# Splitting the experts' up weights into two halves inside the decoder instead of inside the expert loop

## What is computed

```python
x = x + _L0_xattn_ref(_layernorm(x), ctx_1024, ...)   # decoder (self, then cross attention) and feed-forward
x = x + _L0_ffn_ref(_layernorm(x), gate_w, W1, W2, W3) # experts
x = x + _L1_xattn_ref(...)
x = x + _L1_ffn_ref(...)

def _L0_ffn_ref(x, gate_w, W1, W2, W3):
    ...
    h1 = jnp.einsum('td,ehd->teh', xf, W1)     # E, H, D = 8, 896, 256
    h3 = jnp.einsum('td,ehd->teh', xf, W3)
    mid = jax.nn.silu(h1) * h3
    out_all = jnp.einsum('teh,edh->ted', mid, W2)
    ...
```

## Time and profile before

| | us |
|---|---|
| median of 3 runs (1475.7, 1476.38, 1487.08) | 1476.38 |
| the profiled execution | 1489.41 |
| its span, first to last instruction | 1487.7 |

### The profile page before, as it was taken

One profiled execution on the slowest core, in us unless ns is written; L12 is line 12 of the kernel. 1 busy time (PEld: TensorE's weight loads), 2 busy tenths in 40 slices (PEclk: granted clock), 3 DMA queues, 4 the chain that ended last, 5 costly groups with the idle time before them and its releaser, 6 DMA issues. The chain is left out here.

```text
span 1487.7 us, 26152 instructions
## 1 busy us (share of the span) xinstructions
PE 1095.7 (74%) x9362; PEld 734.2 (49%) x9362; DVE 955.5 (64%) x2656; ACT 598.4 (40%) x1195; POOL 413.3 (28%) x579
## 2 busy tenths in 40 slices
PE   2687777777479920399999999940367785899998
PEld 1364444444268820277877777730234432455554
DVE  3646566777337640478888888845367762677776
ACT  1335555666455300366566566510045553000000
POOL 4235654333516637012112112146011100001000
PEclk9768889999889955699999999975579868899999
DMA  7323332422023332666666675326422212010000
GB/s 193 110 68 94 85 92 76 143 80 72 3 85 106 111 111 101 246 215 230 208 242 221 220 243 207 128 85 196 135 67 57 63 32 72 15 39 27 29 8 15
DMA packets 129701, 168.45 MB, mean 113 GB/s; under 512 B 13331, under 2 KB 106278, under 8 KB 126630
## 3 DMA queue, kind: packets, MB, share of 16 engines
q1 hardware_dynamic: 125990, 157.61, 32.6%
q0 software_dynamic: 3584, 9.18, 2.0%
HBM read 119.10 MB, written 47.45 MB: 112 GB/s over the span
## 5 line engine op out<-in xcount | busy, mean ns | idle before, releaser
L1802 PE MATMUL moe_ps_u<-moe_x_hl,moe_up_hl 128*128 128x256 f16 x1932 | 226.5, 276 | 39.9 <-DVE moe_up_hl L1878 31.6
L1802 PEld LDWEIGHTS moe_ps_u<-moe_x_hl,moe_up_hl 128*128 128x128 f16 x1932 | 184.5, 99 | 82.0 <-DVE moe_up_hl L1878 38.0
L2165 PE MATMUL mix_ps_e<-wr_hl,mix_u_hl 128*128 128x512 f16 x768 | 172.4, 380 | 0.0
L1928 POOL CAST moe_mid_hl<-moe_mid 128x256 f16<-128x256 f32 x161 | 68.7, 426 | 312.9 <-DVE moe_mid L1893 312.9
L1878 DVE SCALAR_TENSOR_TENSOR moe_up_hl<-moe_up_in,moe_up_hl 128x512 f16<-128x512 f32 x161 | 105.1, 686 | 54.6 <-ACT moe_up_hl L1851 54.6
L545 ACT ACTIVATE dec_probs<-dec_ps_t 128x768 f32<-128x768 f32 (+1 forms) x128 | 117.2, 916 | 51.5 <-PE dec_ps_t L447 51.1
L2277 DVE SCALAR_TENSOR_TENSOR mix_acc<-mix_ps_e,mix_shares,mix_acc 128x256 f32<-128x256 f32 x256 | 110.3, 477 | 39.3 <-PE mix_ps_e L2165 39.0
L1851 ACT ACTIVATE moe_up_hl<-moe_up_in 128x512 f16<-128x512 f32 x161 | 99.1, 619 | 62.3 <-DMA moe_up_in<-in_moe_w 62.3
L2165 PEld LDWEIGHTS mix_ps_e<-wr_hl,mix_u_hl 128*128 128x128 f16 x768 | 74.9, 98 | 83.3 <-issue 1.1
L1814 PE MATMUL moe_ps_y<-moe_down_hl,moe_mid_hl 128*128 128x256 f16 x966 | 109.0, 273 | 0.0
L1172 DVE TENSOR_REDUCE mem_neg_m<-mem_ps_s 128x2 f32<-128x512 f32 x128 | 82.2, 684 | 38.2 <-PE mem_ps_s L1024 37.5
(11 more groups left out here) (277 smaller groups left out, 1900.8 us busy)
## 6 DMA issues: line engine op xcount, KB each, us to landing
moe_up_in<-in_moe_w SPq DMA_DIRECT2D x23, 1792.0 KB, 7.4
moe_down_in<-in_moe_w SPq DMA_DIRECT2D x23, 896.0 KB, 4.6
dec_q_dram<-dec_q_hl SPq DMA_DIRECT2D x48, 128.0 KB, 2.0
dec_k_dram<-dec_k_hl SPq DMA_DIRECT2D x48, 128.0 KB, 2.0
dec_q_st<-dec_q_dram SPq DMA_DIRECT2D x64, 96.0 KB, 2.6
dec_k_st<-dec_k_dram SPq DMA_DIRECT2D x64, 96.0 KB, 2.6
xs<-zeros SPq DMA_DIRECT2D x8, 736.0 KB
moe_x_in<-xs SPq DMA_DIRECT2D x23, 256.0 KB, 4.3
```

Source lines behind the costliest of these rows:

```text
L1802: mm = nc.tensor.matmul(bank[:, m, :], up_hl[t.slot][:, w, m, dc, f * P:(f + 1) * P], x_hl[t.slot][:, x, dc, :], start=(dc == 0 and w == x ...
L1928: nc.gpsimd.tensor_copy(mid_hl[t.slot][:, HI, f, :], mid[:, f, :]).then_inc(mid_hi, 1)
L2165: mm = nc.tensor.matmul(ps_e[fill % RING][:, :, :], u_hl[t.slot][:, r, dc, k * P:(k + 1) * P], wr_hl[:, m, dc, 2 * q:2 * q + 2, :], start= ...
```

## The change

The up weights of all 8 experts are split once in the decoder, in 64 pieces of 128 x 448, two in each self step and six in each cross step, and stored as halves in a DRAM tensor `moe_hl`. For each piece SP loads it (`load_up`), ACT makes the high half (`up_high`, at the places HIGH_AT), DVE the low half (`up_low`, at LOW_AT), and SP stores both in the next step (`store_up`). In `experts` the split of the up weights is gone from ACT and DVE, `up_in` too; SP loads the halves from `moe_hl` straight into `up_hl`, once `go_up` of the tile that last used the slot is done (`u_filled`). Down weights are split per tile as before. In SP's step the load of the down weights now stands behind that of the up weights.

```diff
 def decoder(...):
+        UP_PIECES, SELF, CROSS = moe_up.shape[2] // PIECE, 2, 6
...
+        UPS, UP_RAWS, UP_SLOTS = ups_before[-1], 9, 8
+        HIGH_AT = {SELF: (2, 4), CROSS: (2, 3, 4, 5, 6, 7)}
+        LOW_AT = {SELF: (3, 5), CROSS: (3, 5, 5, 7, 7, 7)}
...
+                def load_up(n):
+                    if n >= UP_RAWS:
+                        sp.wait_ge(up_lo, n - UP_RAWS + 1)
+                    e, cols = up_at(n)
+                    sp.dma_start(up_raw[n % UP_RAWS][:, :], moe_up[e][:, cols]).then_inc(up_loaded[n % UP_RAWS], 16)
+
+                def store_up(n):
+                    sp.wait_ge(up_lo, n + 1)
+                    e, cols = up_at(n)
+                    sp.dma_start(moe_hl[e][:, :, cols], up_hl[n % UP_SLOTS][:, :, :]).then_inc(up_stored[n % UP_SLOTS], 16)
+
                 for t in STEPS:
...
+                    if within(t - 1):
+                        for n in range(ups_before[t - 1], ups_before[t]):
+                            store_up(n)
+                    if within(t + 1):
+                        for n in range(ups_before[t + 1], ups_before[t + 2])[:CROSS // 2]:
+                            load_up(n)
                     if within(nxt):
                         load_stacks(nxt, 1)
...
                     if within(new):
                         load_stacks(new, 0)
+                    if within(t + 1):
+                        for n in range(ups_before[t + 1], ups_before[t + 2])[CROSS // 2:]:
+                            load_up(n)
...
+                def up_high(n):
+                    act.wait_ge(up_loaded[n % UP_RAWS], 16 * (n // UP_RAWS + 1))
+                    if n >= UP_SLOTS:
+                        act.wait_ge(up_stored[n % UP_SLOTS], 16 * (n // UP_SLOTS))
+                    nc.scalar.activation(up_hl[n % UP_SLOTS][:, HI, :], up_raw[n % UP_RAWS][:, :], ACT.Copy, scale=LIFT).then_inc(up_hi, 1)
...
+                def up_low(n):
+                    dve.wait_ge(up_hi, n + 1)
...
 def experts(...):
                 def step(t):
                     new, ahead, old = t.plus(2), t.plus(3), t.plus(-1)
-                    if new.within():
-                        e = sp.value_load(tile_expert[0:1, bass.ds(new.n, 1)], min_val=0, max_val=E - 1)
-                        if new.before(2):
-                            sp.wait_ge(down_split, HC * (new.n - 1))
-                        sp.dma_start(down_in[new.slot][:, :, :], w2[e]).then_inc(down_loaded[new.slot], 16)
...
                         if ahead.before(2):
-                            sp.wait_ge(up_split, HC * (ahead.n - 1))
-                        sp.dma_start(up_in[ahead.slot][:, :, :, :].rearrange("p m c h -> p (m c h)"), w13[e]).then_inc(up_loaded[ahead.slot], 16)
+                            sp.wait_ge(u_filled, HC * (ahead.n - 1))
+                        sp.dma_start(up_hl[ahead.slot][:, :, :, :, :].rearrange("p l m c h -> p l (m c h)"),
+                                     moe_hl[e]).then_inc(up_loaded[ahead.slot], 16)
+                    if new.within():
+                        e = sp.value_load(tile_expert[0:1, bass.ds(new.n, 1)], min_val=0, max_val=E - 1)
+                        if new.before(2):
+                            sp.wait_ge(down_split, HC * (new.n - 1))
+                        sp.dma_start(down_in[new.slot][:, :, :], w2[e]).then_inc(down_loaded[new.slot], 16)
...
                 def go_up(t):
-                    pe.wait_ge(up_split, HC * (t.n + 1))
+                    pe.wait_ge(up_loaded[t.slot], 16 * (t.turn + 1))
```

More of the change, by code:

```diff
@@ L128, in _, with decoder @@
             pool.wait_ge(done, 11)
-def decoder(nc, c, x, ctx_t, wkv, layers, others, rows, ctx_hl, ctx_dram, table):
+def decoder(nc, c, x, ctx_t, wkv, layers, others, rows, ctx_hl, ctx_dram, table, moe_up, moe_hl):
     with ExitStack() as ctx:
@@ L245, in decoder, with ups_of, up_at @@
         Q_ROWS, K_ROWS = (HI, LO, HI), (HI, HI, LO)
+        UP_PIECES, SELF, CROSS = moe_up.shape[2] // PIECE, 2, 6
+        ups_before = [0]
+        for n in range(ITEMS):
+            ups_before.append(ups_before[-1] + (SELF if causal(n) else CROSS))
+        UPS, UP_RAWS, UP_SLOTS = ups_before[-1], 9, 8
+        HIGH_AT = {SELF: (2, 4), CROSS: (2, 3, 4, 5, 6, 7)}
+        LOW_AT = {SELF: (3, 5), CROSS: (3, 5, 5, 7, 7, 7)}
+        def ups_of(t, places, p):
+            if not within(t):
+                return []
+            first, end = ups_before[t], ups_before[t + 1]
+            return [first + k for k, at in enumerate(places[end - first]) if at == p]
+        def up_at(n):
+            e, k = divmod(n, UP_PIECES)
+            return e, slice(k * PIECE, (k + 1) * PIECE)
+        up_raw = ring(sb, "up_raw", [P, PIECE], n=UP_RAWS)
+        up_hl = ring(sb, "up_hl", [P, 2, PIECE], F16, n=UP_SLOTS)
+        up_loaded, up_stored = ring(sem, "up_loaded", n=UP_RAWS), ring(sem, "up_stored", n=UP_SLOTS)
+        up_hi, up_lo = sem("up_hi"), sem("up_lo")
         params_loaded, ones_set = sem("params_loaded"), sem("ones_set")
@@ L356, in _ @@
                 sp.wait_ge(ctx_stored, 16)
+                for k in range(UP_SLOTS):
+                    sp.wait_ge(up_stored[k], 16 * ((UPS - k + UP_SLOTS - 1) // UP_SLOTS))
             @block.tensor
@@ L598, in _ @@
                             context_high(t + LEAD)
+                        for n in ups_of(t, HIGH_AT, p):
+                            up_high(n)
                         if p == 6:
@@ L718, in _ @@
                             normalise(older)
+                        for n in ups_of(t, LOW_AT, p):
+                            up_low(n)
                         if t == -2:
@@ L1699, in _, with experts @@
                 pool.wait_ge(scattered, 16 * 2 * NT)
-def experts(nc, c, xs, w13, w2, tile_expert, ys, matrices):
+def experts(nc, c, xs, moe_hl, w2, tile_expert, ys, matrices):
     with ExitStack() as ctx:
@@ L1836, in step @@
                             act.wait_ge(y_filled, nxt.n - 1)
-                    if new.within():
-                        act.wait_ge(up_loaded[new.slot], 16 * (new.turn + 1))
-                        if new.before(2):
-                            act.wait_ge(u_filled, HC * (new.n - 1))
                     for f in range(HC):
@@ L1849, in step @@
                                                  scale=LIFT).then_inc(down_hi, 1)
-                        if new.within():
-                            nc.scalar.activation(up_hl[new.slot][:, HI, :, :, f * P:(f + 1) * P].rearrange("p m c h -> p (m c) h"),
-                                                 up_in[new.slot][:, :, :, f * P:(f + 1) * P].rearrange("p m c h -> p (m c) h"), ACT.Copy,
-                                                 scale=LIFT).then_inc(up_hi, 1)
                     if new.within():
                         act.wait_ge(turned, new.n + 1)
+                        if new.before(2):
+                            act.wait_ge(u_filled, HC * (new.n - 1))
                         nc.scalar.copy(x_hl[new.slot][:, HI, :, :], ps_x[:, :, :]).then_inc(x_hi, 1)
@@ L1899, in step @@
                             mid_low(nxt, f - 1)
-                        if new.within() and f % 2 == 1:
-                            up_low(new, f)
                     if nxt.within():
@@ L1907, in step @@
                                                 ALU.subtract).then_inc(x_split, 1)
-                    for f in range(0, HC, 2):
-                        if new.within():
-                            up_low(new, f)
                     n = t.n - 2
@@ L2426, in program @@
             decoder(nc, c, i["x"], i["ctx_t"], i["mem_wkv"], layers, [(i["mem_wq"], mem_wq), (i["w1"], w1_hl), (i["w2"], w2_hl)],
-                    resident, context, ctx_hl, table)
+                    resident, context, ctx_hl, table, i["moe_w13"], moe_hl)
             clear_counted(nc, c)
```

18 lines of the change are left out of this document (8 added, 10 removed).

## The result

The changed kernel takes 1571.1 us (median of 4 runs, 1566.1 to 1582.1), against 1481.7 for the kernel before beside it: a ratio of 1.062, 95% interval 1.058 to 1.066. It is slower, as forecast, but by 89 us instead of 33. The profiled execution took 1571.55 us, its span is 1569.4.

The account below looks back on a forecast made before the run. The prediction took PE to bound the experts and no engine to be full in the decoder's cross steps. Experts +28 us and decoder +5 us took the median from 1476.4 to 1509 us, range 1480 to 1547.

Parts of the forecast that it names:

- The moved down load: Experts: down weights land behind the up load, PE stands 3.0 us per go_up, period 17.4 instead of 15.75 us; experts +28.
- rival 1: Experts: the clock falls in each stall, 1.6 us a tile, 34 us more, 1543 us; chance 0.2.
- The decoder's term: Decoder: splitting 64 pieces costs 0.45 us a cross step and 1 us for all self steps, +5 us together.
- The stacks: Decoder cross steps: stack loads queue behind six stores and three loads, with 3 us of cover; costed at nothing.
- Rival 4: Decoder: late third low half or stacks missing their cover cost some 20 us more, 1530 us; chance 0.1.
- The self steps: Decoder: two pieces in each self step, costed at 1 us in all.
- The freed loop: Experts: without splits on ACT and DVE, PE's own time is 14.4 us a tile, at most 1.35 us less.
- Rivals 2 and 3: Experts: 2, up load doesn't hold up down load, 1471 us, chance 0.14; 3, down load in time, 1446, chance 0.06.

Follow-up runs that it names:

- e1: The change with the down load put back to the head of SP's step, ahead of the wait and the up load: 1451.9 us, 0.982 of the kernel before.
- e3: The kernel before with only the down load moved behind the up load on SP: 1479.5 us, ratio 1.001.
- e6: The change with the down load between the wait for go_up and the up load: 1458.2 us, 0.988 of the kernel before.
- e4: The change with 24 unread matmuls ahead of group 2 in each go_up, filling part of the stall: 1532.6 us, 1.037 of the kernel before.
- e2: The decoder of the change with the experts of the kernel before: 1495.4 us, ratio 1.011.
- e8: e1 with five pieces in each self step, four in each of the first six cross steps, none in the last two: 1461.8 us, 0.990 of the kernel before.
- e12: e1 with the split of a later stage's piece moved to earlier places in the cross steps, on ACT and POOL: 1450.2 us, 0.980 of the kernel before.

## Why the prediction was right in direction and short in size

- **The moved down load: right.** The order, the two landings 2.2 us apart, the silu at the landing and one idle in each `go_up` are as forecast; e1, e3 and e6 show that each link is needed. With the clock held (e4) the period is 17.8 us against 17.4; the landing of the up load, taken as 7.3 us, was 7.1 to 8.1 between the profiled executions (medians from 700 to 800 us; e6, with the down load ahead of it, left out), for the same bytes. Why it varies wasn't tried.
- **The failed step: the clock, rival 1, given 0.2.** "Against it: the idle is shorter, and PE is dense on both sides" was no argument: density didn't protect it. It came true in 17 of 22 tiles, 1.4 to 2.9 us each, 34 us in sum; with the stall filled (e4) the time is 39 us less, and rival 1 had 34. Its price was right, its chance was not, and the range took in rivals 1 and 4 one at a time, while both came. The Trainium skill, "TensorE: Matmul & The Clock Gate", section "HAM oscillation — how this bites in real kernels", tells of a loop whose matmuls wait for a transfer in every tile and start each tile throttled. The traces agree for 17 of the 22 tiles (0.91 with the stall and 1.00 with it filled), not for the other 5.
- **The decoder's term was mis-sized: +17 instead of +5.** Of this the trace of e2 shows 15.6 us. An ordinary cross step costs 0.4 to 0.5 us, as forecast (0.45). Two things were missing. A low half was costed at 0.60 us, scaled from rows of the experts; beside POOL's work it takes up to 1.7 us, and the wait that this makes for PE lets the clock fall here too: some 3.3 and 3.6 us in the three long steps. So rival 1 was missing from this term as well. And the last steps were costed like the others: 6.5 us behind the last rows, which e8, without pieces there, gets back. For 14 us of that stretch PE is at 1.2 GHz in e1; at the same distance from the last rows it is at 2.4 GHz in e3 (which has 4 us at 1.2 GHz later). First e1, then e3:

```profile
371.00:384.00 13.00, 11.78 (x83) 5.42 (x80) 9.30 (x17) 6.79 (x11) 5.46 (x5) 0.50 0.42 109
```

```profile
361.00:375.00 14.00, 10.90 (x136) 5.64 (x136) 9.79 (x22) 9.58 (x14) 6.51 (x7) 1.00 0.00 1
```

  How the 6.5 us divide between the pieces and the clock isn't shown. The stacks, costed at nothing, cost next to nothing in the change's decoder (0.5 us of PE's wait in e2), but only because DVE was late: 3.2 us in e12. Rival 4 had named the place, at 20 us more; 12 more came. The self steps, costed at 1 us, can't be read: item 9's rows stand at 217.0 to 221.1 us in four profiles with the pieces and at 216.8 and 225.6 in the two without.
- **The freed loop: right.** Without the stall a tile takes 14.19 us, forecast as 14.4, instead of 15.75.
- **The sum, as measured:** decoder +17 (e2), stall at full clock 1532.6 - 1478.2 - 17 = +37 (28 forecast; 0.4 us more in 21 periods are 8 of the difference), clock and longer stalls +39. They add up to 93 by construction, as the stall is what the other two leave; the 89 measured has another median of the kernel before (1481.7 for 1478.2). Only the first and the last are measured by runs.
- **Rivals 2 and 3 fell** by the landing times of the change; e6 shows that 3 was one line away. On rival 2 the Trainium skill, "DMA: Bandwidth & Descriptors", section "Queues, rings and completion order", allows another order of completion; in these rows the transfer issued first landed first.

## What to carry to other kernels

When a wait on SP is made later, list what is queued behind it and when that is needed; here one transfer behind the wait and behind 1792 KB cost 119 us, from e1 to the change. A stall inside a dense matmul loop should be priced twice, once for the idle and once for the matmuls behind it at the lower clock. Work put into gaps of another stage costs more than its own length where it runs beside POOL or makes PE stand: look at the granted clock of each step there too. The last steps of this pipeline had no gaps to offer.
